# Eight scatters moved ahead in GpSimd's queue of a one-core attention and expert kernel

## The reference

```python
# layer 1: attention over a random adjacency matrix
h = layernorm(x) @ W.T + b_W
e = (h @ a1)[:, None] + (h @ a2)[None, :] + b_a[0]
e = where(e > 0, e, 0.2 * e)
scores = where(adj > 0, e, -9e15)
x = x + softmax(scores, axis=1) @ h
# layer 2: 64 experts, the best two for each row
xf = layernorm(x)
topk_logits, topk_idx = top_k(xf @ Wr + br, 2)
gates = softmax(topk_logits, axis=1)
for e in range(64):
    y = relu(xf @ W1[e] + b1[e]) @ W2[e] + b2[e]
    out = out + combine[:, e:e+1] * y       # combine holds the two gates
x = x + out
```

## Time and profile before

| | |
|---|---|
| median of 3 runs | 266.3 us |
| the profiled execution | 266.82 us |
| its span in the trace | 265.1 us |
| mean granted TensorE clock | 0.928 |
| TensorE (PE) busy | 222.3 us, 84% |
| VectorE (DVE) busy | 210.0 us, 79% |
| ScalarE (ACT) busy | 182.7 us, 69% |
| GpSimd (POOL) busy | 155.5 us, 59% |
| the 32 scatters, L432 | 40.1 us, 1254 ns each |

### The profile page before, as it was taken

The page is one execution under the profiler, slowest core; times in us unless marked ns, Lnnn a source line. Parts: engine busy times, 40 slices in busy tenths (PEclk is TensorE's granted clock), DMA queues, the critical chain, the costliest instruction groups (busy, mean ns, idle before and its releaser), DMA issues.

```text
span 265.1 us, 6251 instructions
## 1 busy us (share of the span) xinstructions
PE 222.3 (84%) x1863; PEld 212.4 (80%) x1863; DVE 210.0 (79%) x596; ACT 182.7 (69%) x434; POOL 155.5 (59%) x195
## 2 busy tenths in 40 slices
PE   1493999999996999889946469999999999999840
PEld 1353999999996999789925369999999999999730
DVE  6899999999999989999586117888886666676365
ACT  2758979999876889695635238778767777777400
POOL 5780000533578838688787563446888888865600
PEclk9999599999998999999995559999999999999995
DMA  5989764497757861139811132222369410100067
GB/s 150 225 153 172 139 116 82 129 260 200 206 145 133 282 219 80 43 113 422 357 44 53 35 102 62 63 67 66 83 231 305 154 42 31 40 27 30 24 209 276
DMA packets 11120, 36.89 MB, mean 139 GB/s; under 512 B 2256, under 2 KB 2832, under 8 KB 10320
## 3 DMA queue, kind: packets, MB, share of 16 engines
q0 software_dynamic: 5232, 14.98, 24.7%
q1 hardware_dynamic: 5424, 21.11, 23.1%
q10 hardware_dynamic: 432, 0.40, 0.5%
HBM read 39.36 MB, written 5.51 MB: 169 GB/s over the span
## 4 chain that ended last, share of the span: by engine, by line
PE 61%; DVE 21%; DMA 7%; issue 4%; POOL 3%; SPq 1%; ACT 1%; POOLq 0%; DVEq 0%
PE bank L1157 17%; PE bank L1169 16%; PE bank L1050 13%; PE bank L1026 9%; DVE arena L760 5%; DVE arena L754 4%; DMA xs<-in_x 2%; DMA arena<-result 2%; POOL table L432 2%; PE bank L1146 2%; DVE arena L745 1%; PE bank L1069 1%; DVE idx L784 1%; DVE hot L790 1%; DMA rows_in<-table,arena 1%
## 5 line engine op out<-in xcount | busy, mean ns | idle before, releaser
L1050 PE MATMUL bank<-arena 128*128 128x130 f32 x512 | 62.2, 278 | 0.0
L1157 PE MATMUL bank<-arena 128*128 x384 | 60.5, 282 | 0.1
L1050 PEld LDWEIGHTS bank<-arena 128*128 128x128 f32 x512 | 60.3, 194 | 0.2 <-DVE xs L768 0.2
L1169 PE MATMUL bank<-w2s,arena 128*128 x384 | 58.8, 276 | 0.2 <-issue 0.2
L1157 PEld LDWEIGHTS bank<-arena 128*128 128x128 f32 x384 | 51.6, 196 | 0.6 <-issue 0.3
L1169 PEld LDWEIGHTS bank<-w2s,arena 128*128 128x128 f32 x384 | 50.6, 192 | 0.6 <-issue 0.6
L918 DVE SCALAR_TENSOR_TENSOR arena<-bank,arena 128x128 f32 x96 | 33.6, 350 | 21.5 <-PE bank L1169 20.2
L661 ACT ACTIVATE arena<-bank,arena 128x128 f32<-128x128 f32 x96 | 35.2, 367 | 18.3 <-PE bank L1157 16.9
L432 POOL DMA_INDIRECT table<-rows_in,pos x32 | 40.1, 1254 | 10.0 <-issue 8.0
L1026 PE MATMUL bank<-ident,arena 128*128 128x128 f32 x256 | 34.2, 291 | 9.5 <-DVE arena L760 9.5
L911 DVE TENSOR_SCALAR arena<-bank,arena 128x128 f32<-128x128 f32 x96 | 33.3, 346 | 10.1 <-PE bank L1157 9.9
(11 more groups left out here) (196 smaller groups left out, 278.2 us busy)
## 6 DMA issues: line engine op xcount, KB each, us to landing
arena<-in_adj POOLq DMA_DIRECT2D x16, 512.0 KB, 6.6
w2s<-in_w SPq DMA_DIRECT2D x8, 768.0 KB, 4.5
arena<-in_w SPq DMA_DIRECT2D x6, 1024.0 KB
arena<-in_w SPq DMA_DIRECT2D x4, 512.0 KB, 5.3
w2s<-in_w SPq DMA_DIRECT2D x4, 512.0 KB, 3.9
xs<-in_x SPq DMA_DIRECT2D x4, 256.0 KB, 6.3
arena<-result SPq DMA_DIRECT2D x2, 512.0 KB, 4.3
arena<-result SPq DMA_DIRECT2D x4, 256.0 KB, 5.9
```

Of the source, the lines that this page charges most:

```text
L1050: ins = pe.matmul(OB[t % 2][:, 0:D + 2], pt_r[:, t % 2, j, :], h[:, j, :], start=(j == 0), stop=(j == T - 1))
L1157: ins = pe.matmul(hp(p, b), w1u[:, p % UW, P * b:P * b + P], xT_all[:, bass.ds(column, P)], start=True, stop=True)
L1169: ins = pe.matmul(yp(p), hT[:, p % UH, b, :], w2s[:, bass.ds(u, 1), b, :].rearrange("p e d -> p (e d)"), start=(b == 0), stop=(b == HB - 1))
```

## The change

Four tiles' scatters stand further ahead in GpSimd's queue. Tile 3 is scattered at step 12 in place of 13, tile 4 at 13 in place of 14, tile 5 at 14 in place of 15. Tile 9 is scattered ahead of rstd_of(7) in place of behind it; behind rstd_of(7), in its old place with tile 10, now stands tile 11, which was behind rstd_of(8). All other engines' queues are the same.

```diff
-    PLACED = [(0, 0, 10), (0, 1, 11), (0, 2, 12), (0, 3, 13), (1, 4, 14), (1, 5, 15), (1, 6, 15), (1, 7, 15)]
+    PLACED = [(0, 0, 10), (0, 1, 11), (0, 2, 12), (0, 3, 12), (1, 4, 13), (1, 5, 14), (1, 6, 15), (1, 7, 15)]
...
             rstd_of(6)
             place(2, 8)
+            place(2, 9)
             rstd_of(7)
-            place(2, 9)
             place(3, 10)
+            place(3, 11)
             rstd_of(8)
-            place(3, 11)
             for q in range(4, NG):
                 for t in range(START[q], START[q + 1]):
                     place(q, t)
```

## The result

The changed kernel is slower: 268.8 us, the median of 8 runs (267.66 to 270.74), against 266.27 (265.85 to 267.76). The ratio of the runs is 1.0088, with a 95% interval of 1.0052 to 1.0125. Every ratio in this document is to the kernel before, run on the same chip; its medians there differ (267.0 in the experiments), so kernels of different experiments are best compared by their ratios. One run of the version with half of tile 5 and tiles 9 and 11 whole took 282.1 us in a slower state of the chip; it counts in that median and not in the ratio. The profiled execution took 269.17 us with a span of 267.4, where the one before took 266.82 with 265.1. In this execution everything up to 97 us happens about 0.4 us earlier than in the one before: rstd_of(4) begins at 97.29, not 97.70.

What follows compares the result with a forecast made beforehand. GpSimd's scatter backlog was taken to set the experts' start. GpSimd's end 4.1 late less 2.5 is 1.6; with word loads the first `up` is 2.4 late: 266.3 becomes 268.7 us, range 264.8 to 270.8.

Steps and rivals of the forecast that it cites:

- Tile 3 is free: GpSimd, 4.49 us idle ahead of rstd_of(4): tile 3's two scatters fit there and cost nothing.
- Tile 4 gains nothing: GpSimd, step 13: its first scatter, released by `pos`, is held by VectorE's L754, 106.5 to 109.2; no gain.
- Tile 5 brings the stall: GpSimd: tile 5's scatters ahead of rstd_of(5) make it end 6.0 us later; ScalarE's norm(10) is 4.1 late.
- Eight scatters in place of ten give 2.5 us back: GpSimd behind rstd_of(8): two scatters fewer give 2.5 us back, so the padding write is 1.6 us late.
- rival C: Slower still: TensorE's idling brings half clock on tile 14's or 15's products, losing 1.7 us; 270.4 us, chance 0.12.
- The word loads: TensorE behind its table setup: two sets take 4.4 us, putting the first `up` 2.4 us late; 1.6 if hidden.
- The expert pairs are the same work behind this start: Behind the first `up`: the expert pairs' work is unchanged, so the first `up`'s 2.4 us delay carries into the total.
- A: Faster: tile 4's first scatter is not held by L754, rstd_of(5) is through ahead of norm(10); 264.6 us, chance 0.15.
- B: No change: a held scatter gets through at once behind VectorE's end, norm(10) 1.4 us late; 266.2 us, chance 0.18.

Runs made afterwards that it cites:

- the list alone: Changed kernel with tiles 9 and 11 back in their old places, only tiles 3, 4 and 5 a step earlier: 271.45 us, ratio 1.0172.
- the nudge: Two tiny GpSimd copies just ahead of rstd_of(5), added to the kernel with only tile 5's first scatter ahead of it: 268.27 us, ratio 1.0044.

## Why the prediction was right

The forecast was 268.7 us; 268.8 was measured. The prediction speaks of four tiles and eight scatters moved; tile 11 moves too, ahead of rstd_of(8), so it is five tiles and ten scatters. Its sum has tile 11 all the same, in the eight scatters in place of ten behind rstd_of(8). Point by point:

- *Tile 3 is free*: right, it ended 0.9 us ahead of rstd_of(4). *Tile 4 gains nothing*: right, held 2.82 us where 2.7 was forecast, and worth nothing by itself (1.0011). One step came out by luck: its second scatter was to begin ahead of L760, as before, and began 0.02 us inside it; that it still took 0.96 us no row of the prediction had shown.
- *Tile 5 brings the stall*: right in kind and size. L414 took 2.59 where 2.6 was forecast, L417 ended at 118.37 (118.8 net; 118.83 forecast), and ScalarE waited 4.06 us. Without tile 5 the loss is gone.
- *Eight scatters in place of ten give 2.5 us back*: right in size: the padding write is 2.6 us earlier than with the list alone, and 1.7 late net, against 1.6. The reason is narrower than a queue that stays full: tile 9's scatters fill idle time that the stall itself opens ahead of rstd_of(7). And 0.4 of the 1.7 is half clock on tile 14's products, which the forecast left to rival C.
- *The word loads*: wrong in size. I took 4.4 us for TensorE's two sets, from ScalarE's 2.21 for one. No run shows such a time. TensorE's last setup work ended at 151.91 + 1.06 = 152.97 and it transposed at 155.55, so the loads took at most 2.58. In the second trace of the changed kernel TensorE idled 2.58 us in the same place; whether the loads or the gather end there is open. Either way the loads do not end last: the second gather lands at 153.75 + 2.77 = 156.52, its transposes begin at 156.56, and the first `up` is 1.4 later, 1.8 net, where 2.4 was forecast. That is the prediction's own value for loads that are hidden, 1.6, and GpSimd's end sets it.
- *The expert pairs are the same work behind this start*: wrong by 0.85 us. The first `up` is 1.41 later and the last pair 2.26. The granted clock from 156 to 170 us is 0.80 on the mean, and was 0.90 before: half clock for 5.6 us of it, to about 161.6, and for 2.8, to 158.8. Behind the first `up` that is 4.4 us against 3.0, and half of the difference, 0.7, is lost. The profile's row for the changed kernel:

```profile
156.00:170.00 14.00, 13.68 (x100) 13.13 (x99) 7.97 (x28) 10.09 (x31) 6.27 (x7) 0.80 0.25 69
```

So the total came out to 0.1 us partly by luck: a term 0.6 too high met one of about 0.8 that was missing, and the profiled execution was 0.4 ahead before the change began to act. In the second trace of the changed kernel half clock fell where it costs nothing, and the time was 267.67, inside the range that takes in the rivals (264.8 to 270.8) and under the forecast's own (267.9 to 269.8).

The rivals: A (tile 4 not held) and B (a held scatter through at once) did not happen. Behind L760's end at 111.45 the held scatter of 110.38 ended 0.83 us later, as the earlier trace rows had said; the Trainium skill's 115 ns, "SBUF — State Buffer", section "A bandwidth-pool intuition that's wrong (but worth ruling out)", fits neither this nor the 0.58 of L414, and only L417's 0.06 is near it. B's mechanism is real for all that: the nudge made it, and it cost 1.3 us at ScalarE. C (half clock behind TensorE's idle time) came true in kind in both traces, in size in neither: it priced 1.7 us, and the padding write shows 0.4 in one trace and nothing in the other.

## What to carry to other kernels

When a small instruction on a slow queue feeds a critical engine, ask not only how long it will wait but what runs on VectorE at the moment it will start: on which side of a long VectorE instruction it falls can turn 0.3 us into 1.3, and two in a row into 4. The half of a tile fitted ahead of the wait where the whole did not, and gained nothing, since the next instruction was held to the same point. What moving work ahead of a wait gives is the idle time that it fills there: the same two scatters of tile 9 filled 2.64 us behind the stall and 0.43 without it. So ask of such a move how long the queue stands idle at that wait, and whether that idle time is itself a loss that could go.

## What the runs showed of the hardware

How long a held GpSimd instruction runs on behind the end of VectorE's long one depends on what it is, and repeats closely over the thirteen traces: 0.82 to 0.96 us for an indirect DMA, 0.58 to 0.66 for the power on 128x2, 0.04 to 0.06 for the product on 128x2.

The border is sharp, but it does not lie at one place for all. L417 begun 0.13 us ahead of VectorE's instruction took 0.27 us, begun 0.08 behind its start 2.26. An indirect DMA still gets through a little inside: those begun 0.01 to 0.09 us into an L760 took 0.96 to 1.05 us in all thirteen traces, and at 0.09 it was L760 that took longer, 2.41 us in place of 2.35. One begun 0.12 into it, in the kernel with the nudge, took 3.06. At 0.10 both happen; in the kernel with the first scatters of tiles 9 and 11 one was held. Timelines of both engines (L766 is the former L760):

```profile
86.28 2.35 DVE L766 SCALAR_TENSOR_TENSOR arena<-arena,tneg 128x2048 f32<-128x2048 f32 x1
86.38 3.18 POOL L432 DMA_INDIRECT table<-rows_in,pos  x1 [0.17 <-issue]
```

In the changed kernel tile 4's second scatter (109.12, 0.96 us) stands beside this row of VectorE:

```profile
109.10 2.35 DVE L760 SCALAR_TENSOR_TENSOR arena<-arena,tneg 128x2048 f32<-128x2048 f32 x1
```

The place of TensorE's half-clock stretches differs between executions of the same kernel: one trace of the changed kernel has half clock around 83 us and 6.8 us of it behind 120, the other is full at 83 and has 3.4 us from 118.9. The time of a run goes with its mean granted clock. Of the changed kernel's eight runs three had 0.917 or 0.918 (the profiled one is among them) and took 269.17 to 270.74 us; the five with 0.930 to 0.937 took 267.66 to 269.15. The kernel before, 29 runs on one chip, averaged 267.2 us in the fourteen runs under 0.930 and 266.1 in the ten at 0.938 or more. That fits half clock as a reason for the spread of 2 to 3 us between runs; it is not shown to be the only one.
